# Decoder kernel, expert stage: the second layer's weights issued by ScalarE's queue, the first layer's by the sync queue

## The reference

```python
# merged: for each batch element and expert, the weighted sum of the tokens it chose
ones = jnp.ones(merged.shape[:-1] + (1,), merged.dtype)
h = jnp.einsum('bei,eih->beh', jnp.concatenate([merged, ones], -1), w1)   # w1: 32 x 513 x 2048
h = jax.nn.gelu(h, approximate=False)
o = jnp.einsum('bej,ejo->beo', jnp.concatenate([h, ones], -1), w2)        # w2: 32 x 2049 x 512
```

## Time and profile before

| | us |
|---|---|
| median of 3 runs (lowest to highest) | 3848.74 (3847.21 to 3851.14) |
| the profiled execution | 3848.7 |
| its span from first to last instruction | 3846.8 |
| loop of the experts, from the first Gelu's table load to the barrier behind the last store | 1969.7 to 2588.9 |

### The profile page before, as it was taken

How to read it: one execution, slowest core, us unless ns; L and a number is a source line. 1 busy time by engine, 2 the same in 40 slices (tenths; PEclk the granted TensorE clock), 3 DMA queues, 4 the chain that set the end, 5 groups by cost and what they waited for, 6 DMA issues and landing times. The chain is left out here.

```text
span 3846.8 us, 68537 instructions
## 1 busy us (share of the span) xinstructions
PE 3317.9 (86%) x21908; PEld 2304.9 (60%) x21916; DVE 2128.7 (55%) x5418; ACT 1277.9 (33%) x4328; POOL 1423.7 (37%) x2092
## 2 busy tenths in 40 slices
PE   4999999999997999999676656658998799999945
PEld 3776776776774888888421111116776688888821
DVE  5666665665663778787520000005665566766657
ACT  1332232232232555555310000001111466666611
POOL 2555565554561344444200000001222255555537
PEclk9999999999998999999777877878999799999966
DMA  5000000000002111111579999972111211111023
GB/s 131 23 17 16 33 16 16 33 16 21 28 11 78 45 65 44 65 44 55 196 307 426 426 426 427 427 331 84 65 70 48 85 44 62 47 44 65 33 74 131
DMA packets 139587, 440.18 MB, mean 114 GB/s; under 512 B 37408, under 2 KB 40864, under 8 KB 119008
## 3 DMA queue, kind: packets, MB, share of 16 engines
q1 hardware_dynamic: 135424, 435.13, 29.4%
q10 hardware_dynamic: 4096, 4.20, 0.3%
HBM read 392.64 MB, written 46.66 MB: 114 GB/s over the span
## 5 line engine op out<-in xcount | busy, mean ns | idle before, releaser
L436 POOL TENSOR_TENSOR cross_prob<-cross_prob,cross_rsum 128x256 f32<-128x256 f32 (+1 forms) x1024 | 555.1, 568 | 715.2 <-DVE cross_rsum L822 712.4
L675 ACT ACTIVATE cross_prob<-cross_S,cross_neg_max 128x256 f32<-128x256 f32 (+1 forms) x1024 | 445.5, 453 | 137.3 <-DVE cross_neg_max L815 89.7
L436 POOL TENSOR_TENSOR self_prob<-self_prob,self_rsum 128x128 f32<-128x128 f32 (+1 forms) x512 | 249.9, 517 | 228.2 <-DVE self_rsum L822 228.2
L588 PE MATMUL cross_T<-cross_ident,cross_prob 128*128 128x128 f32 x1792 | 292.6, 280 | 15.8 <-DVE cross_probT L827 8.0
L1218 PE MATMUL experts_H<-moe_w,experts_tok 128*32 128x512 f32 x1024 | 164.2, 800 | 134.5 <-DMA moe_b<-in_L_ffn_w 128.6
L588 PEld LDWEIGHTS cross_T<-cross_ident,cross_prob 128*128 128x128 f32 x1792 | 204.8, 142 | 96.7 <-issue 57.4
L675 ACT ACTIVATE self_prob<-self_S,self_neg_max 128x128 f32<-128x128 f32 (+1 forms) x512 | 210.3, 421 | 122.4 <-DVE self_neg_max L815 72.2
L1358 POOL MEMSET norm_minus_half<- 128x2 f32 x1 | 0.1, 104 | 626.3 <-POOLq L53 626.3
L1278 DVE COPY experts_hidT<-experts_T 128x512 f32<-128x512 f32 x32 | 22.1, 691 | 372.3 <-PE experts_T L1229 372.3
L538 PE MATMUL self_A<-self_wo_f,self_zT 128*128 128x512 f32 x512 | 225.2, 593 | 1.6 <-DVE self_res L765 1.0
L675 ACT ACTIVATION_READ_ACCUMULATOR cross_prob<-cross_S,cross_neg_max 128x1 f32 x1024 | 216.6, 211 | 0.0
(11 more groups left out here) (271 smaller groups left out, 8885.3 us busy)
## 6 DMA issues: line engine op xcount, KB each, us to landing
moe_w<-in_L_ffn_w SPq DMA_DIRECT2D x64, 4096.0 KB, 34.6
cross_x_t<-x SPq DMA_DIRECT2D x32, 512.0 KB, 5.1
cross_c_t<-in_ctx SPq DMA_DIRECT2D x32, 512.0 KB, 5.9
cross_res<-x SPq DMA_DIRECT2D x32, 512.0 KB, 3.6
x<-cross_res SPq DMA_DIRECT2D x32, 512.0 KB, 2.8
self_x_t<-in_x SPq DMA_DIRECT2D x16, 512.0 KB, 4.6
self_res<-in_x SPq DMA_DIRECT2D x16, 512.0 KB, 3.6
x<-self_res SPq DMA_DIRECT2D x16, 512.0 KB, 2.8
```

The costliest lines, as they stand in the source:

```text
L436: ins = pool.tensor_tensor(pr, pr, rsum[:, h, t:t + 1].to_broadcast([P, KQ[t]]), ALU.mult)
L588: mm = pe.transpose(TP[:, o:o + P], prob[:, h % NP, SOFF[t] + k * P:SOFF[t] + (k + 1) * P], ident[:, :])
L675: ins = act.activation(prob[:, h % NP, SOFF[t]:SOFF[t] + KQ[t]], SC[h % 4][:, SOFF[t]:SOFF[t] + KQ[t]], ACT.Exp, bias=neg_max[:, h, t:t + ...
```

## The change

ScalarE's part becomes a function, `expert(e, s, last)`. Behind the four stores of expert e it now waits for `o_full` of output(e) and issues w2 of expert e + 2, except for the last two experts, whose code is written out behind the loop; the loop runs 15 times instead of 16. SP's loop keeps the load of w1 and the bias and loses that of w2. The loads of experts 0 and 1 in the route phase stay on SP's queue. TensorE, VectorE and GpSimd are the same.

```diff
@@ sync
                         e = 2 * i + s
                         sp.wait_ge(h_full, e + 1)
                         load_w1(sp, e, s)
-                        sp.wait_ge(o_full, e + 1)
-                        load_w2(sp, e, s)
@@ scalar
-                with act.Fori(0, E // 2) as i:
+                def expert(e, s, last):
+                    act.wait_ge(h_full, 2 + e + 1)
+                    act.wait_ge(ht_full, e + 1)
+                    act.activation(hid[:, s, :], HP[s][:, :], ACT.Gelu).then_inc(act_ok, 1)
+                    act.wait_ge(o_ok, 2 + e + 1)
+                    for n in range(Q):
+                        act.dma_start(out_d[:, n, bass.ds(e, 1), :].rearrange("b o d -> b (o d)"),
+                                      o_sb[32 * n:32 * n + n_batch, s, :]).then_inc(stored[s], 16)
+                    if not last:
+                        act.wait_ge(o_full, 2 + e + 1)
+                        load_w2(act, e + 2, s)
+                with act.Fori(0, E // 2 - 1) as i:
                     for s in range(2):
-                        e = 2 * i + s
-                        act.wait_ge(h_full, 2 + e + 1)
...
+                        expert(2 * i + s, s, False)
+                for s in range(2):
+                    expert(E - 2 + s, s, True)
```

More of the change, by code:

```diff
@@ L1249, in _ @@
                     act.sem_inc(stored[s], 16)
-                with act.Fori(0, E // 2) as i:
-                    for s in range(2):
-                        e = 2 * i + s
-                        act.wait_ge(h_full, 2 + e + 1)
[L1254 to L1259, removed]
+                def expert(e, s, last):
[10 more added lines that the diff above has]
+                with act.Fori(0, E // 2 - 1) as i:
+                    for s in range(2):
+                        expert(2 * i + s, s, False)
+                for s in range(2):
+                    expert(E - 2 + s, s, True)
                 for s in range(2):
```

## The result

| | before | after |
|---|---|---|
| median, us | 3847.97 (8 runs, 3839.07 to 3851.14) | 3863.76 (8 runs, 3856.36 to 3868.30) |
| span of the profiled execution | 3846.8 | 3862.3 |
| expert stage, barrier to barrier | 626.6 | 646.0 |
| last byte of the loads, counted from the stage's start | 617.2 | 631.9 |
| last byte to the start of output(31) | 0.5 | 3.6 |

The change makes the kernel slower: the ratio is 1.0045, with a 95% interval of 1.0033 to 1.0056. That is inside the range of the prediction and far above its likeliest value, 3856.0; it is the time that the prediction gave to the rival in which w2's queue runs dry (3864).

What follows compares the result with a forecast made beforehand. The prediction took the expert loop to be bound by the bytes of its loads. Its terms, 2.4 at the start, 0 in the loop, 3.2 and 1.7 at the tail, summed to +7.3 us, giving 3856.0 us, range 3847 to 3867.

Steps and rivals of the forecast that it cites:

- w2's queue runs dry: Rival, expert loop: gaps of 0 to 0.9 us, up to 14 times, 0 to 12 us on top; 3864, chance 0.19.
- the steady loop: 0 if the engines never run dry: Term for the middle of the expert loop: total work stays 20.3 us an expert, so 0 us.
- the likeliest case: The forecast for the kernel: w1 gets four fifths and runs ahead, sum +7.3 us, 3856.0 us; chance 0.40.
- Rate 0: Term for the expert loads: same bytes through the same 16 full engines, 0 us, bounds -12 to +6 us.
- Turns by runs: Queue sharing in the loop: an engine takes a run from each queue in turn, so w1 gets four fifths.
- The start: Loop's first w2, expert 2: issued later, 2.1 to 2.9 us of engine time lost, +2.4 us.
- The tail: Loop's end: output(31) starts 3.2 us after w2(31) lands and runs 1.7 us longer.
- equal shares: Rival, expert loop: both queues get half, w1 and w2 stay interleaved; +3.3 us, 3852.0, chance 0.20.
- SP's freed time and ScalarE's added work, 0: Issuers in the loop: SP loses and ScalarE gains 30 issues and 30 waits, Gelu not late; 0 us.
- The lone engine: Expert loads: one DMA engine carries the whole 8 KB bias, every landing waits for it; ends 3 us ahead of output(31).

Runs made afterwards that it cites:

- e1: The changed kernel with the load of w2 issued ahead of the four stores on ScalarE's queue; stage 632.9 us, ratio to before 1.0010.
- e5: The changed kernel with w2 of expert e + 2 issued behind the Gelu of expert e + 1; stage 684.4 us, ratio to before 1.0140.
- e2: The changed kernel with w1 read in runs of 8 KB instead of 32 KB; stage 639.8 us, ratio to before 1.0024.
- e6: The kernel before, one queue, with w1 read in 8 KB runs; stage 633.5 us, ratio to before 1.0014.
- e10: The changed kernel with w2 read in runs of 32 KB like w1; stage 629.1 us, ratio to before 0.9998.
- e8: The changed kernel with w2 of experts 2 and 3 issued by SP, all later ones by ScalarE; stage 643.5 us, ratio to before 1.0032.
- e9: The changed kernel with w2 of experts 30 and 31 issued by SP, all others by ScalarE; stage 646.1 us, ratio to before 1.0039.
- e7: The kernel before with all experts' biases loaded once in the route phase, none in the loop; stage 619.5 us, ratio to before 0.9969.
- e11: The changed kernel with the biases loaded once as in e7; stage 642.4 us, ratio to before 1.0028.
- e12: e7 with w2 read in 32 KB runs and first-layer columns and bias in matching order; stage 614.7 us, ratio to before 0.9964.

## Why the prediction was right or wrong

*The direction and the range held, the likeliest case did not.* The step that failed is "the steady loop: 0 if the engines never run dry". They do, once in each pair. The term that I set to 0 measures 10 to 12 us: 0.85 us a pair over 12 pairs of the middle is 10.2, and the 14.7 us by which the last byte is late, less 3.3 for the start, is 11.4.

*The rival had it.* "w2's queue runs dry" gave 0 to 0.9 us a pair and 3864 at 0.6; it was 0.85, and e1 and e5 confirm its mechanism from both sides. That its time, 3864, met the median of 3863.76 is partly luck: with 0.85 its own sum is 14 x 0.85 + 7.3 = 19.2, which is what the stage shows (19.4), and the median moved less because the rest of the program came out shorter. I gave it half the chance of the forecast though I wrote that "the margin is nil by these rows". Its own working was short by one thing. I took 5.5 us from the output's start to its end. The outputs that decide have waited 12 to 16 us for w2, and the granted clock stands at 0.50 then (window 2172 above); they took 5.3 to 6.3 us of matmul time where the earlier trace rows had 5.34, and w2 went out 8.9 us after their start on average (14 outputs, 8.3 to 9.3), not 8.4. The reason that I gave against the rival, that a w1 load would still be in flight, was refuted by my own forecast of w1 being always early.

*Rate 0: right.* e1 leaves it 1.8 us in the whole stage at most, and e2 moves 420 GB/s with two queues where e6 moves 422 with one. The 413 GB/s of the changed kernel from 2140 to 2540 against 426 before are the dry gaps. The rule of the Trainium skill that more issuing queues give no bandwidth ("DMA: Bandwidth & Descriptors", "Issuing engines are not separate DMA queues") held.

*Turns by runs: right*, by e2 and e10. The Trainium skill's other rule (same page, section "Queues, rings and completion order") speaks of turns by packet; with the runs as its packets (the trace has packets of 32,768 B for w1 and 8,192 B for w2) it agrees with the changed kernel, e2 and e10.

*The start: right in cause, short in size.* From 1980 to 2000 the changed kernel moves 356 GB/s, where the full stream has 426: 3.3 us of 20 are lost, not 2.4. The four stores took 2.88 us to issue there, not 1.85, so w2 went out 9.4 us after output(0)'s start (1976.30 to 1985.70) instead of the 8.3 of my sum. That e8 came out 2.5 us lower is near my 2.4 by chance.

*The tail: right in size*, 3.2 + 1.7 forecast, 3.1 + 1.7 in the trace, and 3.7 us less from output(28) on in e9, which takes the exposure away. As e9's whole stage did not gain, this rests on parts of single traces. For equal shares I gave the tail 0 to 1.7 us; e2 has 4.8 us from the last byte to output(31).

*SP's freed time and ScalarE's added work, 0: right.* Gelu was never late: ScalarE had issued w2 at 2151.90 and SP was released by the next hidden layer at 2154.37.

*The lone engine: right in cause (e7), wrong in one expectation.* I expected it to trail at the end as before. In the changed kernel all engines end within a microsecond. The likely reason, which no run shows by itself, is that it catches up in the holes, where the other 15 wait. It fits that without the bias the second queue costs 1.1 us a pair and 22.9 us in all (e11 against e7), more than the 0.85 and 19.4 here.

## What to carry to other kernels

Moving half of a full stream of loads to a second queue adds no bandwidth, and it halves the depth of the stock behind each load: ask for each queue whether its next load is issued before its last one ends while it has the engines to itself, and put that issue ahead of stores and of anything that waits. When two queues compete, the one with the longer contiguous runs gets ahead, and the other one then sets the end. A small one-partition load beside large ones can set every landing, since it falls on one of 16 engines; take it out of the loop.

## What the runs showed of the hardware

- Two full queues share the engines by the lengths of their contiguous runs: with 32 KB against 8 KB the loads landed after 17.2 and 31.0 us (e11), and with equal runs the steps of 14 and 27 us were gone (20.5 us in e2, 17.6 to 22.5 in e10).
- A bias of 8 KB on one partition cost 7.1 us in a stage of 626.6, through one DMA engine that ended some 7 us behind the others (before; 1.4 us in e7, without that load).
- Longer runs were faster in one queue: two outputs took 40.9 us with w1 in 8 KB runs (e6, 2402.70 to 2443.64) against 40.5 in 32 KB, and w2 in 32 KB runs shortened the stage by 4.9 us (e12 against e7; 431 against 427 GB/s from 2140 to 2540).
- TensorE took 6.3 us for the matmuls of an output after a wait of 19 us, and 3.64 us for those of the next one, with little wait ahead of it (e5).
- Just behind a stretch in which the DMA engines had stood almost still, they were busy but slow: a share of 0.89 at 139 GB/s from 1986 to 1987 in the changed kernel, where the full stream has 426.
